# Audio tower: ScalarE makes part of the fp16 high halves by a second gelu pass

## The chip, the cores and the metric

The kernel is one launch on one core of a Trainium2 chip. Times are device microseconds of that core. TensorE is called PE here, VectorE DVE, ScalarE ACT, GpSimd POOL and SyncE SP, as in the profile.

## The reference, cut to what matters

Four clips of 120,000 samples go through six strided convolutions. After each stands a group norm (32 groups of 4 channels) and a gelu in its tanh form. What follows is attention with 12 heads and an expert layer with top-1 choice.

```python
for (cw, cb, gw, gb), (_, _, s) in zip(conv_params, CONV_LAYERS):   # (128,10,5), 4 x (128,3,2), (128,2,2)
    y = conv(h, cw, stride=s) + cb
    yn = (y - mean_of_group) * rsqrt(var_of_group + EPS) * gw + gb
    h = gelu_tanh(yn)
h = h.transpose @ pw.T + pb                # 749 tokens of 192 per clip
h = h + attention(layernorm(h))
h = h + chosen_expert(layernorm(h))        # 8 experts, exact gelu
```

## The kernel before, in words

All engines run their own program in a loop over the four clips ("batches"). In each, the tower comes first (the convolutions, some 150 us), then five passes of a loop over pairs of heads and a last pair, then the work behind attention ("post"). The experts come once, at the end.

**Layout.** Channels are the 128 partitions. A layer's time axis is laid out in rows of 126 columns: 192 rows in layer 0, then 96, 48, 24, 12, 6. A chunk of 8 rows is 1008 columns.

**Two halves.** The convolutions of layers 1 to 5 are fp16 matmuls that need fp32 accuracy. So each activation is kept as a high half (the gelu's value rounded to fp16) and a low half (value minus high half). A bank of 4 output rows is nine matmuls of 504 columns (`terms`, L1680): six on the high half, then three on the low one. PE waits for the high half of a chunk before the first of the nine, and for the low half before the seventh (`hi_done`, `lo_done`).

**PSUM.** `JOBS[TOWER]` is the list of PE's jobs, and each takes one of four slots in turn. Job n may start when the readers of job n-4 have freed its slot (`slot_free`). A conv job is two banks (8 rows), and ACT copies it out in one go (L950, an "eviction"), which frees the slot.

**Layer 0.** A piece is 8 rows of layer 0. There are 24. ACT takes a piece out of PSUM with the gelu (L966) into one of four fp32 stages and so frees the slot. DVE casts it to the high half (L1154) and subtracts to get the low half (L1156). PE makes three pieces, then one or two conv jobs of layer 1, and so on.

**Layers 1 to 4.** When the group norm's scale and bias are there (`affine_ready`), ACT runs `normalise`: one gelu for each chunk of `NORM_CHUNKS`, in place in SBUF (L879). There are 13 chunks in layer 1 (5, 4, ten times 8 and 7 rows), 7 in layer 2, 4 in layer 3, 2 in layer 4. Only behind its last gelu does ACT's program come to the evictions of the next layer's conv jobs. DVE splits the chunks as they come, copies the halo row (L1147, L1148), then takes `bn_stats` of the evicted outputs (L1288, L1284) and aggregates them (L1069) for the next group norm. Layer 2 is made by seven conv jobs: 4, then five of 8, then 4 rows. Layer 3 is made by four, layer 4 by three, layer 5 by one.

**Tables.** The gelu of the tower and the exponential of attention (L893) are in different tables of ACT, so its program has a table load ahead of each.

Of the kernel before, what the change touches and what calls it, by code (L numbers as in the profile page):

```python
# [27 lines left out]
COLS, PITCH = 125, 126  # L28
# [154 lines left out]
def readers(phase, engine):  # L183
# [7 lines left out]
STAGES = 4  # L191


COUNTS = {
    "ps_full": tuple(len(JOBS[f]) for f in PHASES),
    "act_freed": tuple(readers(f, ACT_ENGINE) for f in PHASES),
# [5 lines left out]
    "channel_stats": (1, CONV_LAYERS - 1, 0, 0, 1),  # L202
    "affine_ready": (1, CONV_LAYERS - 1, 0, 0, 1),
    "norm_done": (0, sum(len(c) for c in NORM_CHUNKS.values()), 0, 0, 0),
    "hi_done": (0, len(SPLITS), 0, 0, 0),
    "lo_done": (0, len(SPLITS), 0, 0, 0),
    "halo_done": (0, 4, 0, 0, 0),
    "xn_ready": (0, 1, 0, 0, 1),
# [98 lines left out]
def audio_tower(nc, ins, out):  # L307
# [8 lines left out]
    with ctx:  # L316
# [532 lines left out]
        def _(act):  # L849
# [19 lines left out]
            def normalise(layer, b):  # L869

                wait(act, "affine_ready", TOWER, layer, b)
                r = 0
                for rows in NORM_CHUNKS[layer]:
                    src = ys[layer][:, r * PITCH:(r + rows) * PITCH]
                    dst = src
                    if layer == 5:
                        src = src.rearrange("p (r c) -> p r c", c=PITCH)[:, :, 0:COLS]
                        dst = h5t.rearrange("p (c r) -> p r c", r=rows)
                    a.activation(dst, src, ACT.Gelu_apprx_tanh, bias=affine[:, 1:2], scale=affine[:, 0:1]  # L879
                                 ).then_inc(S["norm_done"], 1)  # L880
                    r += rows
# [57 lines left out]
            with act.Fori(0, BATCH) as b:  # L939
                layer = 0  # L940
                for g, n, kind, args in jobs_of(TOWER):
                    if kind == "conv":
                        if args[0] > 1 and args[1] == 0:
                            normalise(args[0] - 1, b)
                        layer, r, cut = args
                        wait(act, "ps_full", TOWER, n + 1, b)
                        rows = cut[0]
                        dst = ys[layer][:, r * PITCH:(r + sum(cut)) * PITCH]
                        src = slot(g).rearrange("p (k n) -> p k n", k=2)[:, 0:len(cut), 0:rows * PITCH]
                        a.activation(dst.rearrange("p (k n) -> p k n", k=len(cut)), src, ACT.Identity,  # L950
                                     scale=1.0 / WSCALE).then_inc(S["act_freed"], 1)
                    elif kind == "conv0":
                        j, i = args
                        if args == (0, 0):
                            wait(act, "affine_ready", TOWER, 0, b)

                            wait(act, "scratch_stored", TOWER, 0, b)
                        wait(act, "ps_full", TOWER, n + 1, b)
                        piece = 3 * j + i
                        if piece >= STAGES:  # L960

                            had_it = (0, piece - STAGES)
                            wait(act, "hi_done", TOWER, SPLITS.index(had_it) + 1, b)
                            wait(act, "lo_done", TOWER, SPLITS.index(had_it) + 1, b)
                        src = slot(g).rearrange("p (m n) -> p m n", m=2)[:, :, 0:4 * PITCH]
                        a.activation(stage[:, piece % STAGES, :].rearrange("p (m n) -> p m n", m=2), src,  # L966
                                     ACT.Gelu_apprx_tanh,
                                     bias=affine[:, 1:2], scale=affine[:, 0:1]).then_inc(S["act_freed"], 1)
                    elif kind in ("q", "k", "v", "s"):
                        attention_job(TOWER, g, n, kind, args, b)  # L970
                    else:
                        assert kind == "xtr"
                        if layer == 5:
                            normalise(5, b)
                            layer = None
                        wait(act, "ps_full", TOWER, n + 1, b)
                        a.activation(xt_parts[:, args[0], :], bank(g, 0).bitcast(fp16)[:, 0:TOK], ACT.Copy
                                     ).then_inc(S["act_freed"], 1)
                with act.Fori(0, PAIRS - 1) as pr:
                    for g, n, kind, args in jobs_of(PAIR):  # L980
                        attention_job(PAIR, g, n, kind, args, b, pr)
                for g, n, kind, args in jobs_of(LAST_PAIR):
                    attention_job(LAST_PAIR, g, n, kind, args, b)
                for g, n, kind, args in jobs_of(POST):
                    wait(act, "ps_full", POST, n + 1, b)
                    a.activation(xnt1[0:D1, 0:TOK], slot(g)[0:D1, 0:TOK], ACT.Copy).then_inc(S["act_freed"], 1)


            def take_hidden(j, par):
# [19 lines left out]
        def _(dve):  # L1009
# [140 lines left out]
            def split(unit, b):  # L1150

                src, high, low = split_views(*unit)
                n = SPLITS.index(unit) + 1
                v.tensor_copy(high, src).then_inc(S["hi_done"], 1)  # L1154
                dve.wait_ge(S["hi_done"], at("hi_done", TOWER, n, b))
                v.tensor_tensor(low, src, high, ALU.subtract).then_inc(S["lo_done"], 1)  # L1156

            def wait_split(unit, b):
                wait(dve, "hi_done", TOWER, SPLITS.index(unit) + 1, b)
                wait(dve, "lo_done", TOWER, SPLITS.index(unit) + 1, b)  # L1160

            def attention_job(phase, n, kind, args, b, pr=None):
# [284 lines left out]
        def _(pe):  # L1447
# [213 lines left out]
            with pe.Fori(0, BATCH) as b:  # L1661
                for n, (kind, args, who) in enumerate(JOBS[TOWER]):
# [11 lines left out]
                    elif kind == "group":  # L1674
                        wait(pe, "channel_stats", TOWER, args[0], b)
                        last = t.matmul(bank(g, 0)[:, 0:2], group_avg[:, :], ms[:, :], start=True, stop=True)
                    elif kind == "conv":
                        layer, r, cut = args
                        taps = 2 if layer == 5 else 3
                        parts = [a.rearrange("p (r c) -> p r c", c=PITCH) for a in hs[layer - 1]]  # L1680

                        terms = [(tap, w, 0) for tap in range(taps) for w in (0, 1)]
                        terms += [(tap, 0, 1) for tap in range(taps)]
                        for k, c in enumerate(cut):
                            need = 2 * (r + c) - 2 + taps - 1
                            if need >= ROWS[layer - 1]:
                                wait(pe, "halo_done", TOWER, layer, b)
                                need = ROWS[layer - 1] - 1
                            unit = split_unit_of(layer - 1, need)
                            wait(pe, "hi_done", TOWER, SPLITS.index(unit) + 1, b)  # L1690
                            for tap, w, x in terms:
                                if (tap, w, x) == (0, 0, 1):
                                    wait(pe, "lo_done", TOWER, SPLITS.index(unit) + 1, b)
                                f = 2 * r + tap
                                last = t.matmul(bank(g, k)[:, 0:c * PITCH].rearrange("p (r c) -> p r c", c=PITCH),  # L1695
                                                cwt[layer][:, w, tap, :], parts[x][:, f:f + 2 * c - 1:2, :],
                                                start=(tap, w, x) == terms[0], stop=(tap, w, x) == terms[-1])
                            r += c
                    elif kind == "embed":
                        if args[0] == 0:  # L1700
                            wait(pe, "norm_done", TOWER, COUNTS["norm_done"][1], b)
                        tiles = range(4) if args[0] == 0 else range(4, TT)
                        for q, i in enumerate(tiles):
                            m = tile_rows(i)
                            last = t.matmul(bank(g, q // 2)[0:m, (q % 2) * D:(q % 2 + 1) * D],
                                            h5t[:, 128 * i:128 * i + m], pwt[:, :], start=True, stop=True)
                    else:
                        assert kind == "xtr"
                        if args[0] == 0:
                            wait(pe, "xn_ready", TOWER, 1, b)  # L1710
                        for i in range(TT):
                            m = tile_rows(i)
                            last = t.transpose(bank(g, 0).bitcast(fp16)[:, 128 * i:128 * i + m],
                                               xn_parts[0:m, i, args[0], :], ident_h[0:m, 0:m])
# [142 lines left out]
```

## Time and profile before

| | us |
|---|---|
| median of 3 runs | 1816.24 (1814.69 to 1819.27) |
| the profiled execution: its time, its span | 1816.93, 1815.3 |
| PE busy | 1464.7 (81%) |
| DVE busy | 1034.3 (57%) |
| ACT busy | 754.8 (42%) |
| POOL busy | 348.8 (19%) |

The busy shares are means over stages with different limits. The tower is about a third of the span; its first batch lies between 37 and 199 us, with layer 0 up to 101 us and the normalisation of layer 1 from 105.68 us on. The granted clock is TensorE's, as a share of 2.4 GHz.

### The profile page before, as it was taken

To read this page: it belongs to the slowest core of one execution; us is meant where nothing else is said; L and a number is where in the kernel's file an instruction comes from. 1 tells how busy PE (TensorE), PEld (TensorE's weight loads), DVE (VectorE), ACT (ScalarE), POOL (GpSimd) and SP (SyncE) were. 2 spreads that over 40 slices of the span, in tenths; PEclk is the share of its full clock that TensorE was granted. 3 is DMA by queue.
4 is the path that set the end of the run, shared out by engine and by line. 5 is a ranking of instruction groups with operands and counts; after the bars stand their busy time and mean duration, and the time that the engine had idled before them with its cause. 6 is when DMAs were issued, how large, how long until landed. Compare 5 with 4: busy or idle time off the path is not lost.

```text
span 1815.3 us, 32241 instructions
## 1 busy us (share of the span) xinstructions
PE 1464.7 (81%) x10013; PEld 1019.8 (56%) x10014; DVE 1034.3 (57%) x2346; ACT 754.8 (42%) x1456; POOL 348.8 (19%) x390
## 2 busy tenths in 40 slices
PE   4975699998864899989747999898559999159997
PEld 3433477784433677753325777743347778137775
DVE  5987445558884445578964545598744546212221
ACT  2654355525642455435624555265435552012231
POOL 2000134300001334100002333000013331512111
PEclk7987699998986999989878999899769999579999
DMA  4300121210000221110002121100024332621110
GB/s 104 112 1 1 35 60 43 59 36 12 1 1 5 64 59 43 35 38 1 1 1 59 44 59 43 39 1 1 1 57 108 85 86 69 209 56 47 48 50 17
DMA packets 105852, 81.31 MB, mean 45 GB/s; under 512 B 57842, under 2 KB 96267, under 8 KB 105747
## 3 DMA queue, kind: packets, MB, share of 16 engines
q1 hardware_dynamic: 99988, 70.65, 15.5%
q0 software_dynamic: 5760, 9.36, 1.7%
q8 instruction: 54, 0.88, 0.2%
q14 instruction: 50, 0.41, 0.1%
HBM read 34.66 MB, written 18.38 MB: 29 GB/s over the span
## 4 chain that ended last, share of the span: by engine, by line
issue 50%; PE 30%; POOL 7%; DMA 4%; SPq 3%; DVE 3%; ACT 2%; POOLq 0%; DVEq 0%; ACTq 0%
PE ps L1649 5%; PE ps L1591 5%; PE ps L1802 4%; DMA arena<-arena 3%; PE ps L1635 3%; PE ps L1623 3%; PE ps L1782 2%; PE ps L1783 2%; POOL arena L765 2%; PE ps L1598 1%; POOL slot_scratch L824 1%; POOL arena L767 1%; SPq L587 1%; ACT arena L911 1%; PE ps L1790 1%
## 5 line engine op out<-in xcount | busy, mean ns | idle before, releaser
L1695 PE MATMUL ps<-arena,cwt 128*128 128x504 f16 (+2 forms) x1776 | 396.3, 387 | 62.1 <-DVE arena L1154 61.8
L1695 PEld LDWEIGHTS ps<-arena,cwt 128*128 128x128 f16 x1776 | 181.1, 104 | 268.3 <-DVE arena L1154 69.2
L1176 DVE TENSOR_REDUCE nmax<-ps 128x1 f32<-128x128 f32 (+5 forms) x288 | 176.9, 614 | 195.7 <-PE ps L1626 195.7
L1649 PE MATMUL ps<-arena 128*128 128x64 f32 (+2 forms) x2016 | 260.1, 269 | 9.1 <-DVE arena L1184 5.0
L1649 PEld LDWEIGHTS ps<-arena 128*128 128x128 f32 (+2 forms) x2016 | 241.9, 189 | 26.0 <-issue 17.8
L1156 DVE TENSOR_TENSOR arena<-arena 128x1008 f16<-128x1008 f32 (+4 forms) x200 | 227.0, 1135 | 6.9
L1184 DVE COPY arena<-ps 128x512 f32<-128x512 f32 (+4 forms) x288 | 156.1, 542 | 85.8 <-PE ps L1635 81.4
L893 ACT ACTIVATE arena<-ps,nmax 128x128 f32<-128x128 f32 (+5 forms) x288 | 180.8, 628 | 44.1 <-DVE nmax L1176 43.3
L1623 PE MATMUL ps<-arena 128*128 128x512 f16 (+6 forms) x780 | 164.6, 314 | 42.4 <-DMA arena<-arena 21.5
L1635 PE MATMUL ps<-ident,arena 128*128 128x128 f32 (+2 forms) x1008 | 165.8, 282 | 10.6 <-ACT arena L934 5.7
L950 ACT ACTIVATE arena<-ps 128x1008 f32<-128x1008 f32 (+1 forms) x112 | 96.3, 867 | 179.4 <-PE ps L1695 179.4
L934 ACT ACTIVATE arena<-ps,rinv 128x64 f32<-128x64 f32 (+1 forms) x288 | 91.0, 316 | 162.2 <-PE ps L1649 159.1
L879 ACT ACTIVATE arena<-arena,affine 128x1008 f32<-128x1008 f32 (+5 forms) x108 | 113.2, 1125 | 92.8 <-DVE affine L1092 92.8
L1154 DVE CAST arena<-arena 128x1008 f16<-128x1008 f32 (+4 forms) x200 | 128.2, 641 | 28.2 <-ACT arena L879 16.1
L1635 PEld LDWEIGHTS ps<-ident,arena 128*128 128x128 f32 (+2 forms) x1008 | 109.7, 144 | 49.2 <-ACT arena L934 38.4
L756 POOL TENSOR_TENSOR tmp<-tmp,neg_half 128x1 f32<-128x1 f32 x25 | 13.9, 555 | 625.7 <-DVE tmp L1082 625.7
L1623 PEld LDWEIGHTS ps<-arena 128*128 128x128 f16 (+2 forms) x780 | 76.1, 118 | 76.2 <-DMA arena<-arena 24.8
L1288 DVE BATCH_NORM_STATS2 bn<-arena 128x6 f32<-128x500 f32 (+1 forms) x180 | 103.0, 630 | 19.8 <-ACT arena L950 19.7
L966 ACT ACTIVATE arena<-ps,affine 128x1008 f32<-128x1008 f32 x96 | 107.2, 1193 | 0.6 <-DVE arena L1156 0.4
L992 ACT ACTIVATE arena<-ps 128x768 f32<-128x768 f32 x31 | 25.2, 812 | 195.4 <-PE ps L1783 195.4
L765 POOL TENSOR_TENSOR arena<-arena,ones_col 128x750 f16<-128x750 f32 x40 | 57.4, 1435 | 189.5 <-ACT arena L911 189.5
L1591 PE MATMUL ps<-arena,w_parts 128*128 128x375 f16 x288 | 69.0, 353 | 9.4 <-ACT arena L893 6.5
(249 smaller groups left out, 2060.5 us busy)
## 6 DMA issues: line engine op xcount, KB each, us to landing
arena<-arena SPq DMA_DIRECT2D x96, 187.5 KB, 3.0
arena<-arena SPq DMA_DIRECT2D x96, 93.8 KB, 2.6
slot_scratch<-empty_slot SPq DMA_DIRECT2D x1, 5775.0 KB, 19.1
arena<-in_L_ffn_w SPq DMA_DIRECT2D x8, 576.0 KB
arena<-in_L_ffn_w SPq DMA_DIRECT2D x8, 384.0 KB
arena<-slot_scratch SPq DMA_DIRECT2D x31, 96.5 KB, 1.9
arena<-slot_scratch SPq DMA_DIRECT2D x31, 96.0 KB, 2.0
xa<-in_x POOLq DMA_DIRECT2D x5, 468.8 KB, 4.3
```

What stands on the lines that cost most here:

```text
L879: a.activation(dst, src, ACT.Gelu_apprx_tanh, bias=affine[:, 1:2], scale=affine[:, 0:1]).then_inc(S["norm_done"], 1)
L893: a.activation(prob[k % PROBS][0:m, 0:128 * i + m], slot(g)[0:m, 0:128 * i + m], ACT.Exp, bias=nmax[0:m, k_:k_ + 1], accum_out=rsum[0:m, k ...
L966: a.activation(stage[:, piece % STAGES, :].rearrange("p (m n) -> p m n", m=2), src, ACT.Gelu_apprx_tanh, bias=affine[:, 1:2], scale=affine ...
L1154: v.tensor_copy(high, src).then_inc(S["hi_done"], 1)
L1156: v.tensor_tensor(low, src, high, ALU.subtract).then_inc(S["lo_done"], 1)
L1176: v.reduce_max(nmax[0:m, k_:k_ + 1], slot(g)[0:m, 0:128 * i + m], AX.X, negate=True).then_inc(S["smax_done"], 1)
L1184: v.tensor_copy(probt[k % 2][:, 0:w, 0:m], src[:, 0:w, 0:m]).then_inc(S["dve_freed"], 1)
L1591: last = t.matmul(bank(g, k)[:, 0:TOK // 2], weights, x, start=m == 0, stop=m == len(terms) - 1)
L1623: last = t.matmul(slot(g)[0:m, lo:hi], q, keys[:, lo:hi], start=a == 0, stop=a == len(terms) - 1 and not diagonal)
L1635: last = t.transpose(slot(g)[0:kk, 128 * c:128 * c + m], prob[k % PROBS][0:m, 128 * c:128 * c + kk], ident[0:m, 0:m])
L1649: last = t.matmul(slot(g)[0:m, Z_AT:Z_AT + DH], probt[k % 2][0:kk, c, 0:m], vt[0:kk, c, DH * hh:DH * hh + DH], start=c == 0, stop=c == i)
L1695: last = t.matmul(bank(g, k)[:, 0:c * PITCH].rearrange("p (r c) -> p r c", c=PITCH), cwt[layer][:, w, tap, :], parts[x][:, f:f + 2 * c - 1 ...
```

## The change

ACT makes the high half of some chunks itself: a gelu pass with fp16 output straight into the high half, ahead of the pass with fp32 output that it makes anyway. DVE then only subtracts. `hi_engine` says who does it: in layer 0 ACT for pieces 0, 1, 2 and every third one from 3 on (10 of 24), in layers 1 to 4 ACT for chunks 0, 2, 4 and so on (7 of 13, 4 of 7, 2 of 4, 1 of 2). The semaphore `hi_done` becomes two, `hi_act` and `hi_dve`, and PE waits for both. At the end of a batch ACT gets a gelu of one column, whose result nobody reads.

```diff
+def hi_engine(layer, piece):
+    if layer == 0:
+        return ACT_ENGINE if piece < 3 or piece % 3 == 0 else DVE_ENGINE
+    return DVE_ENGINE if piece % 2 else ACT_ENGINE
+def highs(engine, unit):
+    return sum(hi_engine(*u) == engine for u in SPLITS[:SPLITS.index(unit) + 1])
...
+                    elif hi_engine(layer, piece) == ACT_ENGINE:
+                        a.activation(split_views(layer, piece)[1], src, ACT.Gelu_apprx_tanh, bias=affine[:, 1:2],
+                                     scale=affine[:, 0:1]).then_inc(S["hi_act"], 1)
                     a.activation(dst, src, ACT.Gelu_apprx_tanh, bias=affine[:, 1:2], scale=affine[:, 0:1]
                                  ).then_inc(S["norm_done"], 1)
...
                             had_it = (0, piece - STAGES)
-                            wait(act, "hi_done", TOWER, SPLITS.index(had_it) + 1, b)
                             wait(act, "lo_done", TOWER, SPLITS.index(had_it) + 1, b)
                         src = slot(g).rearrange("p (m n) -> p m n", m=2)[:, :, 0:4 * PITCH]
+                        if hi_engine(0, piece) == ACT_ENGINE:
+                            a.activation(split_views(0, piece)[1],
+                                         src.rearrange("p m (k c) -> p m k c", c=PITCH), ACT.Gelu_apprx_tanh,
+                                         bias=affine[:, 1:2], scale=affine[:, 0:1]).then_inc(S["hi_act"], 1)
...
+                a.activation(spare[:, 30:31], ones_col[:, :], ACT.Gelu_apprx_tanh)
...
-                v.tensor_copy(high, src).then_inc(S["hi_done"], 1)
-                dve.wait_ge(S["hi_done"], at("hi_done", TOWER, n, b))
+                if hi_engine(*unit) == DVE_ENGINE:
+                    v.tensor_copy(high, src).then_inc(S["hi_dve"], 1)
+                    dve.wait_ge(S["hi_dve"], at("hi_dve", TOWER, highs(DVE_ENGINE, unit), b))
+                else:
+                    dve.wait_ge(S["hi_act"], at("hi_act", TOWER, highs(ACT_ENGINE, unit), b))
                 v.tensor_tensor(low, src, high, ALU.subtract).then_inc(S["lo_done"], 1)
...
-                            wait(pe, "hi_done", TOWER, SPLITS.index(unit) + 1, b)
+                            wait(pe, "hi_act", TOWER, highs(ACT_ENGINE, unit), b)
+                            if highs(DVE_ENGINE, unit):
+                                wait(pe, "hi_dve", TOWER, highs(DVE_ENGINE, unit), b)
```

ACT between the last eviction of layer 1 and the first of layer 2, before (L879 is the gelu of `normalise`, L950 the eviction):

```order
L879 ACTIVATE arena<-arena,affine 128x630 [waits affine_ready]
L879 ACTIVATE arena<-arena,affine 128x504
L879 ACTIVATE arena<-arena,affine 128x1008 x10
L879 ACTIVATE arena<-arena,affine 128x882
L516 REGISTER_ALU
L950 ACTIVATE arena<-ps 128x504 [waits ps_full]
```

The same place now (L893 is the added pass, L895 the old one, L966 the eviction):

```order
L893 ACTIVATE arena<-arena,affine 128x630 [waits affine_ready]
L895 ACTIVATE arena<-arena,affine 128x630
L895 ACTIVATE arena<-arena,affine 128x504
L893 ACTIVATE arena<-arena,affine 128x1008
L895 ACTIVATE arena<-arena,affine 128x1008 x2
...
L893 ACTIVATE arena<-arena,affine 128x882
L895 ACTIVATE arena<-arena,affine 128x882
L529 REGISTER_ALU
L966 ACTIVATE arena<-ps 128x504 [waits ps_full]
```

Where 13 gelus stood ahead of the first eviction, 20 stand now.

ACT at the head of the loop over the batches, now (L982 is the added pass in layer 0, L985 the old one; L529 holds the waits):

```order
L529 ISA [waits affine_ready]
L529 ISA [waits scratch_stored]
L982 ACT_TABLE_LOAD
L982 ACTIVATE arena<-ps,affine 128x2x4x126 [waits ps_full]
L985 ACTIVATE arena<-ps,affine 128x1008
```

And at the end of the loop's body, now (L1007 is the gelu of one column):

```order
L1005 ACTIVATE arena<-ps 64x750
L1007 ACT_TABLE_LOAD
L1007 ACTIVATE spare<-ones_col 128x1
L955 REGISTER_ALU
L955 COMPARE_AND_BRANCH
```

The load at the loop's end is new. The one at its head, behind the wait for `affine_ready`, stands where it stood before.

## Rows read from the trace of the kernel before

**Rows 1.** Who PE waited for, whole span: us in total, times, longest.
```profile
PE ps L1676 <- DVE ms L1071: 62.3, 20, 5.8
PE ps L1695 <- DVE arena L1154: 61.8, 20, 3.4
```
**Rows 2.** Layer 0, batch 0: us; busy PE, PEld, DVE, ACT, POOL; clock; DMA share; GB/s.
```profile
38.00:102.00 64.00, 58.12 (x256) 24.32 (x256) 57.98 (x75) 39.20 (x38) 0.00 (x0) 0.92 0.34 106
```
**Rows 3.** Timeline of DVE, layer 1 normalised: start us, us, what [idle before].
```profile
106.62 0.49 DVE L1154 CAST arena<-arena 128x630 f16<-128x630 f32 x1 [0.98 <-ACT arena L879]
107.15 0.81 DVE L1156 TENSOR_TENSOR arena<-arena 128x630 f16<-128x630 f32 x1
...
136.38 0.53 DVE L1069 BATCH_NORM_AGGREGATE mv<-bn 128x2 f32<-128x84 f32 x1
```
**Rows 4.** Timeline of PE, the same stretch.
```profile
107.17 24.43 PE L1695 MATMUL ps<-arena,cwt 128*128 128x252 f16 x117 [3.25 <-DVE arena L1154]
```
**Rows 5.** Timeline of ACT, the same stretch.
```profile
105.68 13.82 ACT L879 ACTIVATE arena<-arena,affine 128x630 f32<-128x630 f32 x13 [4.49 <-DVE affine L1092]
119.40 2.36 ACT L950 ACTIVATE arena<-ps 128x504 f32<-128x504 f32 x3
122.07 1.01 ACT L950 ACTIVATE arena<-ps 128x1008 f32<-128x1008 f32 x1 [0.31 <-PE ps L1695]
125.90 1.01 ACT L950 ACTIVATE arena<-ps 128x1008 f32<-128x1008 f32 x1 [2.81 <-PE ps L1695]
...
131.64 0.59 ACT L950 ACTIVATE arena<-ps 128x504 f32<-128x504 f32 x1 [0.90 <-PE ps L1695]
```
**Rows 6.** Forms between 105 and 170 us: count, busy us, mean ns.
```profile
L879 ACT ACTIVATE arena<-arena,affine 128x1008 f32<-128x1008 f32 x15 | 17.1, 1214 | 0.0
L1154 DVE CAST arena<-arena 128x1008 f16<-128x1008 f32 x15 | 10.2, 678 | 0.0
...
L879 ACT ACTIVATE arena<-arena,affine 128x882 f32<-128x882 f32 x3 | 3.3, 1111 | 0.0
L879 ACT ACTIVATE arena<-arena,affine 128x630 f32<-128x630 f32 x3 | 2.7, 913 | 15.8 <-DVE affine L1092 15.8
...
L879 ACT ACTIVATE arena<-arena,affine 128x504 f32<-128x504 f32 x3 | 2.4, 793 | 0.0
```
**Rows 7.** Two reads of one PSUM slot by ACT, fp16 then fp32 out.
```profile
203.71 0.89 ACT L909 ACTIVATE arena<-ps,bqkv 128x750 f16<-128x750 f32 x1 [3.85 <-PE ps L1591]
204.50 0.88 ACT L911 ACTIVATE arena<-ps,bqkv 128x750 f32<-128x750 f32 x1
```
**Rows 8.** Stretches of 1 us, PE idle; the granted clock stands third from the end.
```profile
133.00:134.00 1.00, 0.00 (x0) 0.00 (x0) 1.00 (x3) 0.00 (x0) 0.00 (x0) 0.85 0.00 0
134.00:135.00 1.00, 0.00 (x0) 0.00 (x0) 1.00 (x2) 0.00 (x0) 0.00 (x0) 0.50 0.00 0
```
**Rows 9.** Timeline of PE, first conv job of layer 1, batches 0 and 1.
```profile
44.45 5.92 PE L1695 MATMUL ps<-arena,cwt 128*128 128x504 f16 x18 [2.29 <-DVE arena L1154]
...
423.03 5.69 PE L1695 MATMUL ps<-arena,cwt 128*128 128x504 f16 x18 [2.36 <-DVE arena L1154]
```
**Rows 10.** Timeline of PE, the convolution of layer 3.
```profile
141.23 13.27 PE L1695 MATMUL ps<-arena,cwt 128*128 128x252 f16 x63 [3.24 <-DVE arena L1154]
```
**Rows 11.** Timeline of DVE, the same stretch: the aggregation behind the last bn_stats.
```profile
155.94 0.37 DVE L1069 BATCH_NORM_AGGREGATE mv<-bn 128x2 f32<-128x48 f32 x1
```
**Rows 12.** Timeline of ACT in layer 0, batch 0, and its start in batch 1.
```profile
38.80 6.60 ACT L966 ACTIVATE arena<-ps,affine 128x1008 f32<-128x1008 f32 x6
...
55.58 1.01 ACT L950 ACTIVATE arena<-ps 128x1008 f32<-128x1008 f32 x1 [0.92 <-PE ps L1695]
...
416.79 5.52 ACT L966 ACTIVATE arena<-ps,affine 128x1008 f32<-128x1008 f32 x5
```
**Rows 13.** ACT in batch 1; then all loads of L966: ns min/median/max.
```profile
415.49 1.28 ACT L966 ACT_TABLE_LOAD   x1 [10.94 <-DVE affine L1092]
...
L966 ACT ACT_TABLE_LOAD  x4: 1283/1283/1283, 37.5 to 1173.1; - x4
```

More of the change, by code:

```diff
@@ L204 @@
     "norm_done": (0, sum(len(c) for c in NORM_CHUNKS.values()), 0, 0, 0),
-    "hi_done": (0, len(SPLITS), 0, 0, 0),
+    "hi_act": (0, sum(hi_engine(*u) == ACT_ENGINE for u in SPLITS), 0, 0, 0),
+    "hi_dve": (0, sum(hi_engine(*u) == DVE_ENGINE for u in SPLITS), 0, 0, 0),
     "lo_done": (0, len(SPLITS), 0, 0, 0),
@@ L872, in normalise @@
                 r = 0
-                for rows in NORM_CHUNKS[layer]:
+                for piece, rows in enumerate(NORM_CHUNKS[layer]):
                     src = ys[layer][:, r * PITCH:(r + rows) * PITCH]
@@ L1152, in split @@
                 src, high, low = split_views(*unit)
-                n = SPLITS.index(unit) + 1
-                v.tensor_copy(high, src).then_inc(S["hi_done"], 1)
-                dve.wait_ge(S["hi_done"], at("hi_done", TOWER, n, b))
+                if hi_engine(*unit) == DVE_ENGINE:
[3 more added lines that the diff above has]
+                    dve.wait_ge(S["hi_act"], at("hi_act", TOWER, highs(ACT_ENGINE, unit), b))
                 v.tensor_tensor(low, src, high, ALU.subtract).then_inc(S["lo_done"], 1)
             def wait_split(unit, b):
-                wait(dve, "hi_done", TOWER, SPLITS.index(unit) + 1, b)
+                if hi_engine(*unit) == ACT_ENGINE:
+                    wait(dve, "hi_act", TOWER, highs(ACT_ENGINE, unit), b)
                 wait(dve, "lo_done", TOWER, SPLITS.index(unit) + 1, b)
```

## The prediction

> **What bounds the kernel now.** I read the waits first, then the busy time by stretch, then the timeline of each engine over the first batch's tower. In the waits [rows 1] two groups of 20 belong to the tower: 62.3 us in which PE waits for DVE's statistics and 61.8 us for DVE's casts. So DVE looks like the engine to relieve. The stretches show where that holds. In layer 0 [rows 2] PE is busy 58.12 of 64.00 us and DVE 57.98. Once PE has begun its first conv job at 44.45 it never waits there, so PE sets the pace and DVE, though nearly full, is just behind. In the normalisation of layer 1, DVE sets the end: from the first cast at 106.62 to the aggregation at 136.38 it has no gap (first cast and aggregation stand in [rows 3]), while PE was done at 107.17 + 24.43 = 131.60 [rows 4] and then waited. ACT has its 13 gelus done at 105.68 + 13.82 = 119.50 [rows 5]. That is before the fifth of seven conv jobs of layer 2 needs the first one's slot: evictions of full jobs follow each other by 125.90 - 122.07 = 3.83 us, so a matmul of 504 columns takes 3.83 / 18 = 0.213 us, and jobs five to seven are 45 of them, 9.57 us. They began at 131.55 - 9.57 = 121.97, and the first slot was free by about 120.
>
> **The change, part by part.** Sums are made against the profiled execution, 1816.93 us (span 1815.3), 0.7 us over the median of 1816.24.
>
> *Layer 1, the casts that go.* DVE loses seven of 13 casts: about 0.5 + 5 x 0.68 + 0.6 = 4.5 us [rows 3, 6]. If DVE stayed the bound, this would be the gain.
>
> *Layer 1, the passes that come.* ACT gets seven passes: 0.913 + 5 x 1.214 + 1.111 = 8.09 us of durations [rows 6]. Back to back they overlap: 13 gelus have 0.913 + 0.793 + 10 x 1.214 + 1.111 = 14.96 us of durations and take 13.82 [rows 5], 0.095 us for each. That leaves 7.43 us. No row shows this gelu with an fp16 output. The nearest are two reads of one slot, 0.89 us in fp16 and 0.88 in fp32 [rows 7], so I take no difference. The last gelu ends at 119.50 + 7.43 = 126.93, and the first eviction, about 0.5 us later, at 127.45. The fifth job needs that slot. PE, ready at 121.97, waits 5.5 us. This is what is queued behind the added passes: seven evictions on ACT, on them PE's jobs five to seven, on these DVE's `bn_stats`.
>
> *The clock.* After PE stopped at 131.6 the granted clock went from 1.00 to 0.85 in the stretch 133 to 134 and to 0.50 from 134 on, which is 1.2 instead of 2.4 GHz [rows 8]. So I expect it at 1.2 GHz when job five begins. What the way back costs: 18 matmuls after such a stop took 5.69 to 5.92 us against 3.83 [rows 9], a loss of about 1.9. After the stop at 107.17, 117 matmuls took 24.43 us [rows 4]; the last 99 are 99 x 0.213 = 21.05 us, so the first 18, of half width, took 3.4 against 1.9, a loss of 1.5. I take 1.7, and 0 as the lower bound.
>
> *The end of the stage.* PE ends at 127.45 + 9.57 + 1.7 = 138.7. DVE has caught up by then. Behind a PE that ends last, the aggregation comes 155.94 - (141.23 + 13.27) = 1.44 us later [rows 10, 11]. So it comes at 140.16 instead of 136.38: +3.8 us a batch, and +2.1 if the clock costs nothing.
>
> *The early start.* PE may begin on the high half that ACT makes at about 106.6, not at 107.17. But the low half of chunk 0 now waits for ACT's second pass, to 107.4, and for 0.81 us of subtraction [rows 3], while six matmuls at 1.2 GHz last 1.3 us. So PE stops again in front of the seventh, and bank 2 ends where it ended. I count 0. The same holds in layers 2 to 4.
>
> *Layers 2 to 4.* They have four conv jobs, three and one behind them, so all slots are free and no eviction is waited for. ACT's added four, two and one passes end before PE does. The last chunk's halves come up to 0.5 us later in layer 3. I take +0.3 us for all three, with -0.5 and +1.5 as bounds.
>
> *Layer 0, start.* ACT runs gelus in PSUM at a step of (6.60 - 1.19) / 5 = 1.08 us [rows 12]. The first conv job is job 6 and needs the slot of piece 2, which is free after the sixth pass now, not after the third: 38.80 + 6.60 = 45.4 against 44.45 before, +1.0 us. In batches 1 to 3 the first conv job began later anyway, 423.03 - 416.79 = 6.24 us after ACT [rows 9, 12]; there it is +0.4.
>
> *Layer 0, inside.* Removed casts give nothing, since PE sets the pace. ACT makes one more pass, 1.08 us, for every three pieces, where it had 0.92 us of idle time plus 0.1 of overlap ahead of the eviction at 55.58 [rows 12]. Evictions come 0.05 to 0.1 us late, and behind single conv jobs PE waits for them: +0.15 us a batch, 0 to +1.
>
> *The table load.* Before each tower 1.28 us of table load stand behind `affine_ready`, on the path in each of four batches [rows 13]. ACT's order shows that this load stays at the head of the loop, and that the gelu of one column adds a second one at its end. That one runs in ACT's idle time ahead of the head, 10.94 us in batch 1, so it costs nothing. It also gives nothing: the load at the head is an instruction in the program and runs whatever table is in. The Trainium skill ("ScalarE: Activation LUTs", step-by-step on the table-load gate) says that the compiler has put a load in front of an activation if its set isn't active, which read alone would promise that the load goes. The page "ScalarE activation tables: per-element evaluation and per-set limits" (table sets in the compiler) says that loads are placed per block; by this rule the loop's body is given its own, and ACT's order agrees.
>
> *Waits.* PE's extra waits stand ahead of matmuls that queue behind others, and cost nothing while PE's queue is full.
>
> *Sum.* Layer 1: 4 x 3.8 = 15.2. Layer 0: 1.0 + 3 x 0.4 + 4 x 0.15 = 2.8. Layers 2 to 4: 1.2. Together +19.2 us: 1836.1 in the profile's terms, 1835 as a median.
>
> **The rivals.**
> - *The clock doesn't fall in the new stop, or costs nothing.* For it: the stop of 5.5 us is short, and its place against the fall seen 2.2 us after 131.6 may differ. Against: [rows 8]. Then 4 x 1.7 less: 1828.5.
> - *The touch works.* The load at the head is passed over, or takes no time, where the gelu table is already in. No row shows a load of a table that is in; all four took 1283 ns. Then three batches gain 1.28 us each: 1831.
> - *Faster: DVE's relief wins in layer 1.* If ACT's added passes cost so little that the first eviction comes before 121.97, PE ends at 131.6, the aggregation 1.44 us later at 133.0, and each batch gains 3.4 us: with layer 0 as above, about 1816 - 13.6 + 2.8 = 1805. The balance is where PE ends at 134.9: at added ACT work of some 5.4 us without the clock's loss and 3.7 with it. I reckon with 7.4, so the passes would have to cost half of what these rows say.
> - *Only the sizes differ.* If the fp16 pass with rows of 126 columns is slower than the fp32 one by 10%, layer 1 grows by 0.8 us a batch: 1838.5 and more, up to 1842 with layer 0.
>
> **How the numbers follow.** Chances: the forecast, with its sizes, 0.64; no loss by the clock 0.14; the touch works 0.10; slower sizes 0.06; faster 0.03; effects that cancel, within 0.3%, 0.03. A change of 0.3% (5.4 us) is about what a measurement of this kernel can tell from none. Slower by more than that: 0.94. The range reaches from 1823 (no loss by the clock, and layer 0 without its start) to 1842.
>
> **What would show it.** In the changed kernel's timeline of ACT, 20 passes after layer 1's affine take about 21.2 us. PE's conv stretch of layer 2 is in two parts with a stop near 5.5 us between job four and five, ended by an ACT eviction, and the clock is 0.50 at the start of the second part. PE waits for ACT evictions for some 22 us in all, where before there are none of that kind. The table load at the head of each batch is there, 1283 ns long, eight of the gelu kind instead of four, and ACT's first gelu begins 1.3 us behind the affine. DVE's casts fall by 24 a batch. It is wrong if PE's jobs five to seven follow without a stop, or if the head's loads are gone.

## The result, and the profile after

The changed kernel takes 1842.91 us, the median of 4 runs (1841.21 to 1847.80). The kernel before takes 1815.92 in the runs beside them. The ratio is 1.015, with an interval of 1.0126 to 1.0174: 27 us slower (23 to 32), where 19.2 were forecast. 1842.9 lies 0.9 us above the range's upper end. In the profiled execution (1841.21 us, span 1839.6) it is +24.3 us of span. A total can hide which of its terms were wrong, so each is looked up below.

The page's busy row after; against before DVE is down by 54 us and ACT up by 101:

```profile
PE 1488.9 (81%) x10013; PEld 1022.9 (56%) x10014; DVE 980.3 (53%) x2250; ACT 856.2 (47%) x1560; POOL 348.4 (19%) x390
```

PE's waits after (us in total, times, longest). The first two answer to [rows 1]; the third line is new:

```profile
PE ps L1700 <- DVE ms L1092: 50.0, 20, 2.8
PE ps L1721 <- ACT arena L893: 44.0, 16, 2.8
PE ps L1721 <- ACT arena L966: 17.4, 4, 5.3
```

PE's timeline after, layer 1 normalised and layer 2 convolved, batches 0 and 1. It answers to [rows 4]:

```profile
107.83 1.44 PE L1721 MATMUL ps<-arena,cwt 128*128 128x252 f16 x6 [2.73 <-ACT arena L893]
109.57 13.89 PE L1721 MATMUL ps<-arena,cwt 128*128 128x252 f16 x66 [0.30 <-DVE arena L1179]
128.79 11.31 PE L1721 MATMUL ps<-arena,cwt 128*128 128x504 f16 x45 [5.33 <-ACT arena L966]
...
492.69 15.17 PE L1721 MATMUL ps<-arena,cwt 128*128 128x252 f16 x66 [0.30 <-DVE arena L1179]
511.92 12.58 PE L1721 MATMUL ps<-arena,cwt 128*128 128x504 f16 x45 [4.06 <-ACT arena L966]
```

The one stretch of 117 matmuls is now in three parts: six matmuls on the high half from ACT, 66 more, and behind a stop of 5.33 us the 45 of jobs five to seven. ACT's timeline, the same stretch of batch 0, and DVE's aggregation behind it, show what ends the stop. They answer to [rows 5] and [rows 3, 11]:

```profile
106.86 0.91 ACT L893 ACTIVATE arena<-arena,affine 128x630 f16<-128x630 f32 x1 [4.41 <-DVE affine L1113]
...
126.97 1.11 ACT L895 ACTIVATE arena<-arena,affine 128x882 f32<-128x882 f32 x1
127.98 3.25 ACT L966 ACTIVATE arena<-ps 128x504 f32<-128x504 f32 x4
```
```profile
141.54 0.53 DVE L1090 BATCH_NORM_AGGREGATE mv<-bn 128x2 f32<-128x84 f32 x1
```

ACT's 20 passes run from 106.86 to 128.08, 21.22 us. Only then comes its first eviction, and PE starts again 0.81 us after that one began. PE ends at 128.79 + 11.31 = 140.10, and the aggregation follows 1.44 us later.

The granted clock at PE's new stop, in stretches of 1 us (columns: from and to, length, PE busy with its instructions, clock, DMA share, GB/s); batch 0, then batch 1:

```profile
127.00:128.00 1.00, 0.00 (x0) 1.00 0.00 0
128.00:129.00 1.00, 0.21 (x1) 0.81 0.00 0
129.00:130.00 1.00, 1.00 (x3) 0.50 0.00 0
132.00:133.00 1.00, 1.00 (x6) 0.99 0.00 0
...
510.00:511.00 1.00, 0.00 (x0) 0.95 0.00 0
...
517.00:518.00 1.00, 1.00 (x5) 0.64 0.00 0
518.00:519.00 1.00, 1.00 (x6) 1.00 0.00 0
```

In batch 0 the clock falls from 1.00 to 0.50, to 1.2 GHz, only while PE starts again, and is back at 132, after 3.2 us of matmuls. In batch 1 it falls during the stop, and comes back only shortly before 518, after 5.8 us of matmuls. The same 45 matmuls take 11.31 us there and 12.58 here, against the forecast's 9.57 at 2.4 GHz.

Stage lengths tell where the rest is. They are differences between DVE's writes of `affine`, summed over the four batches (us; "elsewhere" is the span less these, all in code that the change leaves alone):

| kernel | layer 0 | layer 1 | layers 2-4 | elsewhere | span |
|---|---|---|---|---|---|
| before | 274.1 | 136.3 | 174.6 | 1230.3 | 1815.3 |
| after | 278.5 | 155.6 | 179.2 | 1226.4 | 1839.6 |
| touch at the end | 274.4 | 136.3 | 174.5 | 1230.7 | 1815.8 |
| touch at the head | 272.2 | 136.3 | 177.9 | 1228.5 | 1814.8 |
| only layer 1 | 274.8 | 152.4 | 173.8 | 1228.6 | 1829.5 |
| the same, PE kept warm | 274.1 | 145.4 | 177.7 | 1233.2 | 1830.3 |
| only layer 0 | 281.3 | 136.3 | 176.4 | 1235.7 | 1829.7 |
| layer 0's start | 278.5 | 136.3 | 179.6 | 1229.1 | 1823.5 |
| layer 0's inside | 273.8 | 136.6 | 178.1 | 1228.9 | 1817.3 |
| only layers 2-4 | 274.3 | 136.3 | 176.7 | 1226.8 | 1814.0 |
| all but layer 0 | 274.1 | 152.7 | 179.1 | 1227.0 | 1832.9 |
| early evictions | 273.1 | 138.0 | 176.2 | 1229.2 | 1816.5 |
| whole change mended | 274.3 | 138.1 | 178.9 | 1226.9 | 1818.1 |
| four passes, early eviction | 273.0 | 128.6 | 182.6 | 1232.0 | 1816.2 |
| PE filled | 273.3 | 135.5 | 169.4 | 1228.2 | 1806.4 |
| both | 273.8 | 127.8 | 170.8 | 1229.8 | 1802.2 |

Two things are to be seen. Layer 1 carries most of the loss. And stages that a kernel's edit doesn't touch move by up to 8 us in sum, so small differences in one stage's sum, or in the span of one execution, show nothing.

### The profile page after: what moved, and what is told of

Same layout as the page of the kernel before. It is cut to its first block, busy times and chain, and to the rows that moved or that the text cites. A ratio compares the mean times of both kernels' runs of the same rounds, so it can differ in the third digit from the quotient of the medians.

```text
span 1839.6 us, 32421 instructions
## 1 busy us (share of the span) xinstructions
PE 1488.9 (81%) x10013; PEld 1022.9 (56%) x10014; DVE 980.3 (53%) x2250; ACT 856.2 (47%) x1560; POOL 348.4 (19%) x390
## 4 chain that ended last, share of the span: by engine, by line
issue 51%; PE 30%; POOL 7%; DMA 4%; SPq 3%; DVE 3%; ACT 2%; POOLq 0%; DVEq 0%; ACTq 0%
PE ps L1673 5%; PE ps L1615 5%; PE ps L1828 3%; DMA arena<-arena 3%; PE ps L1647 3%; PE ps L1659 3%; PE ps L1808 2%; PE ps L1809 2%; POOL arena L778 2%; PE ps L1622 1%; POOL slot_scratch L837 1%; POOL arena L780 1%; SPq L600 1%; ACT arena L927 1%; PE ps L1816 1%
## 5 line engine op out<-in xcount | busy, mean ns | idle before, releaser
L1721 PE MATMUL ps<-arena,cwt 128*128 128x504 f16 (+2 forms) x1776 | 417.3, 399 | 73.4 <-ACT arena L893 44.0
L950 ACT ACTIVATE arena<-ps,rinv 128x64 f32<-128x64 f32 (+1 forms) x288 | 90.8, 315 | 162.7 <-PE ps L1673 158.9
L966 ACT ACTIVATE arena<-ps 128x1008 f32<-128x1008 f32 (+1 forms) x112 | 95.4, 866 | 123.2 <-PE ps L1721 123.0
L895 ACT ACTIVATE arena<-arena,affine 128x1008 f32<-128x1008 f32 (+5 forms) x108 | 116.7, 1123 | 16.6 <-DVE affine L1113 16.6
L985 ACT ACTIVATE arena<-ps,affine 128x1008 f32<-128x1008 f32 x96 | 108.5, 1202 | 0.0
L893 ACT ACTIVATE arena<-arena,affine 128x1008 f16<-128x1008 f32 (+3 forms) x56 | 62.7, 1120 | 64.3 <-DVE affine L1113 64.3
L927 ACT ACTIVATE arena<-ps,bqkv 128x750 f32<-128x750 f32 x48 | 42.5, 885 | 75.2 <-PE ps L1659 39.4
```

## The experiments

My theory: ACT's evictions stand in its program behind the added passes, and PE's jobs wait for them; the clock's fall adds to it. Rivals: the passes themselves or contention cost; the table touch matters; the loss is in layer 0. The edits are shown shortened to the lines that matter, and dots stand for what is left out.

**The touch alone**, at the loop's end as in the change, and instead at its head. Both are before plus one line:

```
+ a.activation(spare[:, 30:31], ones_col[:, :], ACT.Gelu_apprx_tanh)   # end of the loop's body
```


> The kernel before with the gelu of one column at a batch's end, nothing else. My theory: the load at the head of the loop stays, 1283 ns behind the affine in each of four batches, and the added load lies in idle time: same time as before, within 1 us. Rival (the touch works): three batches gain 1.28 us each, 3.8 us less. Second rival (the touch is among the causes of the 24 us): 1 us or more slower.

```
  with act.Fori(0, BATCH) as b:
+     a.activation(spare[:, 30:31], ones_col[:, :], ACT.Gelu_apprx_tanh)
```


> The kernel before with the same gelu of one column as ACT's first instruction in the loop's body, ahead of the wait for the affine. My theory: a load is placed once per block, so it moves in front of the wait; ACT is idle there (4.9 us in batch 0, 10.9 later): four times 1.28 us less, about 1811. Rival: the time between affine and first conv job is set by another engine, and the gain is under 2 us.

At the end: 1817.49, ratio 0.9993 (0.9982 to 1.0004). At the head: 1815.13, 0.9985 (0.9975 to 0.9995). ACT's timelines at the start of batch 1, touch at the end, then at the head:

```profile
405.09 1.28 ACT L988 ACT_TABLE_LOAD   x1
...
416.00 1.28 ACT L966 ACT_TABLE_LOAD   x1 [9.42 <-DVE affine L1094]
417.30 5.52 ACT L966 ACTIVATE arena<-ps,affine 128x1008 f32<-128x1008 f32 x5
```
```profile
408.94 1.28 ACT L941 ACT_TABLE_LOAD   x1 [3.62 <-issue]
...
417.67 6.60 ACT L967 ACTIVATE arena<-ps,affine 128x1008 f32<-128x1008 f32 x6 [7.24 <-PE ps L1672]
```

At the end, the head's load is still there and takes its 1.28 us though the gelu table is in. This is the Trainium skill's rule of loads placed per block ("ScalarE activation tables: per-element evaluation and per-set limits", table sets in the compiler), and the trace agrees. At the head the load moves into idle time, and the first gelu waits for PE instead. So the whole gain is 0.15% or 2.7 us (0.9 to 4.5), not the 5.1 that were expected of four loads. In the profiled execution layer 0's stage is 1.5 us shorter in batch 0 and 0.0 to 0.3 in the others.

**Layer 1 alone**: the changed kernel with ACT's share in one layer, without the touch.

```
- return DVE_ENGINE if piece % 2 else ACT_ENGINE
+ return ACT_ENGINE if layer == 1 and piece % 2 == 0 else DVE_ENGINE
```


> The changed kernel with ACT's added passes in layer 1 alone (7 chunks; no pass in layers 0 and 2 to 4, no touch). Theory A, the stop of PE behind the fourth conv job and the slow clock after it carry the loss: layer 1's stage is 4.0 to 5.1 us longer a batch, 16 to 20 us in all, 1832 to 1836. Rival B, the loss above the forecast's 3.8 in batches 1 to 3 came over from layer 0's changed timing: 15 us in all, 1831. Rival C, the loss is spread over all layers: under 10 us.

1831.47, ratio 1.0072 (1.0056 to 1.0087). Layer 1's stages are 38.12, 38.06, 38.17 and 38.01 us against 34.06 to 34.08: +4.0 in every batch, where 3.8 was forecast. PE's timeline in batch 1:

```profile
511.38 11.31 PE L1721 MATMUL ps<-arena,cwt 128*128 128x504 f16 x45 [5.32 <-ACT arena L966]
```

This is batch 0 of the changed kernel again. So the 12.58 us and the shorter stop of its batch 1 don't come from layer 1's own edit.

**The same with PE kept warm**, that is busy, so that the clock stays up: PE repeats the nine matmuls of job four's second bank twice, which changes no result and shortens its stop (again over the kernel with layer 1 alone).

```
+ for again in range(2 if (layer, r, k) == (2, 24, 1) else 0):
+     for tap, w, x in terms:
+         last = t.matmul(...)
```


> The kernel with ACT's passes in layer 1 alone, in which PE repeats the last bank of layer 2's fourth conv job twice (18 matmuls of 504 columns, 3.83 us at 2.4 GHz, same result), so that it works through most of the stop. Theory A: job five starts at the same time, on ACT's eviction, but at 2.4 GHz, so layer 1's stage costs only 2.2 us a batch over the kernel before, 9 us in all, about 1825. Rival: if the slow matmuls behind the stop don't come from the stop, the time is that of layer 1 alone, 1832 to 1836, or more if the repeats are in the way.

1829.96, ratio 1.006 (1.0044 to 1.0076). PE's timeline in batch 1:

```profile
502.00 3.99 PE L1727 MATMUL ps<-arena,cwt 128*128 128x504 f16 x18
507.48 9.73 PE L1721 MATMUL ps<-arena,cwt 128*128 128x504 f16 x45 [1.50 <-ACT arena L966]
```

PE begins job five at the same place behind ACT's passes, but at 2.4 GHz or nearly so: 9.73 us instead of 11.31. Layer 1 costs +2.2 us a batch instead of +4.0, so the split of the 3.8 into queue and clock (2.1 and 1.7) holds. Yet the whole time is hardly better, and not the 1825 expected: in the profiled executions the 7.0 us gained in layer 1 come back as 3.9 in layers 2 to 4 and 4.6 elsewhere (this kernel's profiled execution is 2.1 us over its median).

**The queue taken away**: as layer 1 alone, but three evictions are written between the passes.

```
+ if layer == 1 and piece in (8, 10, 12):
+     evict(first + (8, 10, 12).index(piece), ...)
```


> ACT's seven passes in layer 1 alone, but ACT evicts the first three conv jobs of layer 2 between its gelus, behind chunks 8, 10 and 12, not behind the last. Theory A, the queue behind the passes is the cause: the same added work on ACT, but the slot of the first job is free before PE wants it, no stop, and layer 1's stage is at most 1 us longer than before (ACT's last gelu comes at 22.7 us, DVE's seven us of statistics behind it), so 1816 to 1820. Rival: the passes themselves are the cost (ACT's pace per chunk, or contention for SBUF), and the time stays at 1831.

1818.63, ratio 1.0003 (0.9994 to 1.0013). PE's and DVE's timelines in batch 1:

```profile
488.84 23.74 PE L1737 MATMUL ps<-arena,cwt 128*128 128x252 f16 x111 [0.31 <-DVE arena L1194]
```
```profile
506.73 0.69 DVE L1190 CAST arena<-arena 128x1008 f16<-128x1008 f32 x1 [0.71 <-ACT arena L907]
507.45 1.21 DVE L1194 TENSOR_TENSOR arena<-arena 128x1008 f16<-128x1008 f32 x1
508.84 1.08 DVE L1194 TENSOR_TENSOR arena<-arena 128x882 f16<-128x882 f32 x1 [0.19 <-ACT arena L907]
```

The stop is gone, and with it the loss: +0.44 us a batch is left. All seven passes are still there, so in themselves they cost no more than that; the order of ACT's program does. But nothing is gained from DVE's relief either, since DVE now waits for ACT's gelus up to the last chunk.

**Layer 0 alone**, then only its first three pieces, then only the pieces inside:

```
+ return ACT_ENGINE if layer == 0 and (piece < 3 or piece % 3 == 0) else DVE_ENGINE   # layer 0
+ return ACT_ENGINE if layer == 0 and piece < 3 else DVE_ENGINE                       # start
+ return ACT_ENGINE if layer == 0 and piece > 5 and piece % 3 == 0 else DVE_ENGINE    # inside
```


> The changed kernel with ACT's passes in layer 0 alone (10 of 24 pieces, no touch). Theory: layer 0's stage is longer as in the changed kernel, 0.4 to 1.9 us a batch, and the others are as before: 1817 to 1822. What came over from layer 0 to layer 1 in the changed kernel needs a stop in layer 1, which isn't there, so layer 1 stays at 34.1 us a batch. Rival: relief of DVE pays in layer 0, and the stage is shorter.

> ACT's added passes for pieces 0, 1 and 2 of layer 0 alone. With all ten pieces, layer 0's stage was 1.6 to 1.95 us longer a batch. Theory: that is the start. The first conv job needs the slot of piece 2, freed by ACT's sixth pass and not its third (0.8 to 1.0 us), and the clock comes back to 2.4 GHz about 1.1 us of work later, so nearly all of it is here: 1.5 to 1.9 us a batch in layer 0, 6 to 7.6 us in the sum of its stages. Rival: the start costs the forecast's 0.4 to 1.0, and the rest is ACT's pace inside the layer: 2.5 us in the sum.

> ACT's added passes for pieces 6, 9, 12, 15, 18 and 21 of layer 0 alone, none at its start. Theory: an eviction behind every third piece comes 0.05 to 0.1 us late, and layer 0's stage grows by 0.1 to 0.3 us a batch, about 1 us in all: not to be told from the kernel before. Rival: the rest of layer 0's loss is here, 1 us or more a batch, 1822.

Layer 0 alone: 1831.04, ratio 1.0065 (1.0049 to 1.0082). Start: 1825.14, 1.0038 (1.0025 to 1.0051). Inside: 1817.49, 1.0003 (0.9994 to 1.0013). The inside costs nothing, the start does, and layer 0 is far over the forecast. But start and inside come to 7 and 0.5 us against 12, a gap of 4 to 5 us that is at the edge of the errors. Piece 3 is ACT's in the change and in neither of the two parts, and no run has it alone. PE's timeline with layer 0 alone, first conv job of batch 2, with the granted clock of the stretches; then before:

```profile
808.91 6.75 PE L1721 MATMUL ps<-arena,cwt 128*128 128x504 f16 x18 [1.22 <-ACT arena L985]
```
```profile
808.90:812.00 3.10, 3.09 (x8) 0.50 0.00 0
812.00:814.00 2.00, 2.00 (x7) 0.50 0.00 0
814.00:815.00 1.00, 1.00 (x5) 0.74 0.00 0
```
```profile
801.80 5.69 PE L1695 MATMUL ps<-arena,cwt 128*128 128x504 f16 x18 [2.32 <-DVE arena L1154]
```
```profile
801.80:805.00 3.20, 3.20 (x10) 0.64 0.00 0
805.00:806.00 1.00, 1.00 (x4) 0.50 0.00 0
806.00:807.00 1.00, 1.00 (x6) 0.93 0.00 0
```

The table load that opens the batch began at 800.50 here and at 794.23 before, so the job starts 8.41 us behind it instead of 7.57: +0.84. And it lasts 1.06 us longer, at 1.2 GHz nearly throughout, where before a part ran faster. Together 1.9, which is what the stage is longer by (70.5 against 68.6). Batches 0 and 1 have jobs of 6.31 and 6.79 us. With the start alone, batch 2's job stands 8.03 us behind its load, +0.46 (0.4 were forecast), and lasts 5.95 us; the rest of the +0.84 is ACT's first gelu, which waits 0.40 us for PE in the kernel with layer 0 alone.

Of +14.4 us of span layer 0 holds 7.2, layers 2 to 4 hold 1.8 and code elsewhere 5.4: every batch's attention and remainder is 233.4 to 233.5 us instead of 232.1 to 232.4. The clock explains at most half of that. Added up over stretches of 2 us, the time at 1.2 GHz is 35.5 us a batch instead of 34.4, and 1.1 us at half the speed loses 0.6 us of work. In the kernel called "whole change mended" the same stretch of batch 3 is shorter, 231.05 us, with 36.5 us at 1.2 GHz.

**Layers 2 to 4 alone, and all but layer 0**:

```
+ return ACT_ENGINE if layer > 1 and piece % 2 == 0 else DVE_ENGINE     # layers 2 to 4
```


> The changed kernel with ACT's passes in layers 2 to 4 alone. In the changed kernel these stages were 4.5 us longer over four batches, where the forecast had 1.2. Theory: it is their own cost, the later low halves and the later halo row, so 4 to 5 us here, about 1821. Rival: it was the clock's state left by the stop in layer 1, and here they cost 1 us or less.


```
  if layer == 0:
-     return ACT_ENGINE if piece < 3 or piece % 3 == 0 else DVE_ENGINE
+     return DVE_ENGINE                                                 # the rest as in the change
```


> The whole change less ACT's passes in layer 0 (layers 1 to 4 and the touch stay). Theory A: layer 0's timing set the clock's state in layer 1, so layer 1's stage is 4.0 us longer than before in every batch and not 5.1, layers 2 to 4 cost 0 to 2 us in all, and the kernel is near 1830. Rival B: layer 1 at 5.1 us comes from the passes in layers 2 to 4 or the touch, and stays: 1835 or more.

Layers 2 to 4 alone: 1816.33, ratio 0.9991 (0.9982 to 1.0001), nothing where 4 to 5 us were expected. All but layer 0: 1832.7, ratio 1.0076 (1.0059 to 1.0092), and layer 1's stages are back at 38.17, 37.94, 38.44 and 38.10. So what makes them 39.1 to 39.2 in batches 1 to 3 of the changed kernel is the edit in layer 0, a stage earlier. Layers 2 to 4 stay at 179.1, as in the changed kernel, so what these stages have over before does not come from layer 0's edit.

**The whole change with both waits mended**: pieces 0 to 3 back to DVE, three evictions early in layer 1.

```
- return ACT_ENGINE if piece < 3 or piece % 3 == 0 else DVE_ENGINE
+ return ACT_ENGINE if piece > 5 and piece % 3 == 0 else DVE_ENGINE
+ if layer == 1 and piece in (8, 10, 12): evict(...)
```


> The whole change with both suspected waits taken away: in layer 0 ACT makes high halves only from piece 6 on (pieces 0 to 3 are DVE's again), and in layer 1 the first three evictions stand behind chunks 8, 10 and 12. 20 of 24 added passes a batch stay. Theory A: the two waits are all of it, so 1816 to 1820. Rival B: the passes have a cost of their own, spread out: 1825 or more.

1818.39, ratio 1.000 (0.999 to 1.001). The two places on ACT are the whole loss, within 0.1%; the other 20 of 24 added passes a batch cost nothing that can be measured. In layer 1 this is shown for the order alone, with every pass kept. In layer 0 the passes themselves went, four of them, so there the queue is the explanation that fits the rows, and not shown apart from the passes.

**A better split**: touch at the head, only chunks 4, 6, 8 and 10 of layer 1 on ACT, one eviction early.

```
+ return ACT_ENGINE if layer == 1 and piece in (4, 6, 8, 10) else DVE_ENGINE
+ if layer == 1 and piece in (9,): evict(...)
```


> A version meant to win: the touch at the head of the loop's body, ACT's passes in layer 1 for four chunks alone (4, 6, 8, 10), and the first conv job of layer 2 evicted behind chunk 9. By the terms measured so far: DVE loses 4 x 0.71 us of casts in layer 1 and stays the bound, ACT ends its gelus at 18.8 us and isn't waited for, so 2.7 us less a batch, 10.8 in all, and 3 for the touch: about 1804. Rival: PE's or ACT's pace takes the bound at once and layer 1 gives nothing: 1815.

1817.56, ratio 0.9993 (0.9984 to 1.0002). Layer 1 is shorter by 1.9 us in each batch, as DVE's casts leave its path, and the sum is still nothing, not the 1804 expected: 7.7 us gained there, 7.9 lost in layers 2 to 4. PE's timeline of the next convolution, batch 1, this kernel and before:

```profile
514.49 0.59 PE L1716 MATMUL ps<-ms,group_avg 128*128 128x2 f32 x2 [3.51 <-DVE ms L1108]
518.32 14.31 PE L1738 MATMUL ps<-arena,cwt 128*128 128x252 f16 x63 [3.24 <-DVE arena L1191]
```
```profile
515.72 0.59 PE L1676 MATMUL ps<-ms,group_avg 128*128 128x2 f32 x2 [5.53 <-DVE ms L1071]
519.55 13.27 PE L1695 MATMUL ps<-arena,cwt 128*128 128x252 f16 x63 [3.24 <-DVE arena L1154]
```

The same 63 matmuls come 1.2 us earlier and take 1.04 us more, at the lower clock for longer (7.2 us instead of 5.6 in this stage, added up over stretches of 1 us). This stage takes 19.2 to 20.5 us in these kernels, also where nothing near it was edited: with the touch at the head it is 20.55 us in batch 0, with 7.8 us at the lower clock, and 19.4 in the others. Here all four batches are near the upper end.

**PE filled**: around the matmul that averages the statistics PE does others whose result nobody reads, so that it doesn't idle there; over the kernel with the touch at the head, and over the last one.

```
+ for again in range((0, 9, 20, 7, 7, 0)[layer]):     # (0, 9, 12, 7, 7, 0) over the last one
+     t.matmul(bank(g, 1)[:, 0:4 * PITCH], cw0t[:, 0, :], xt[:, 0:4, :]...)
  wait(pe, "channel_stats", ...); last = t.matmul(..., group_avg, ms)
+ for again in range((0, 11, 11, 11, 11, 0)[layer]): ...
```


> The kernel before with the touch at the head, in which PE does matmuls whose results nobody reads (504 columns, into the unused bank of the group job's slot) while it waits for statistics and for the first high half of layers 1 to 4. Theory: PE's slow matmuls at the start of layers 3, 4 and 5's convolutions (some 1.0, 2.0 and 1.0 us a batch) are the clock's alone, so they go, and the stages of layers 2 to 4 are 3 to 5 us shorter a batch: about 1799. The stage of layer 1 stays, DVE sets it. Rival: the slow stretch is the cost of starting a job, not of idling before it, and nothing moves: 1815.

> The same filling in the version with ACT's passes for four chunks of layer 1, which was 1.9 us a batch shorter in layer 1 and gave it all back in layers 2 to 4 (1.1, 0.6 and 0.2 us a batch), with the clock at 1.2 GHz for 7.3 to 7.8 us of layer 2's stage where it had been 5.4 to 5.8. Theory: with the clock held up, layer 1's gain stays: 7 us under the filled kernel, about 1792. Rival: the give-back has another cause and stays: the two are equal.

The first: 1812.32, ratio 0.9978 (0.996 to 0.9995), with runs spread from 1807.18 to 1821.79. The second: 1802.95, ratio 0.9911 (0.9897 to 0.9926), 14.4 us under the kernel before by the medians (13 to 19 by the interval) and 40 under the changed one: it beats both. PE's timeline of it, batch 1:

```profile
504.82 2.71 PE L1717 MATMUL ps<-xt,cw0t 105*128 105x504 f16 x12
509.00 0.39 PE L1720 MATMUL ps<-ms,group_avg 128*128 128x2 f32 x2 [1.47 <-DVE ms L1108]
509.25 3.56 PE L1723 MATMUL ps<-xt,cw0t 105*128 105x504 f16 x11
512.63 10.39 PE L1747 MATMUL ps<-arena,cwt 128*128 128x252 f16 x54
523.87 2.09 PE L1747 MATMUL ps<-arena,cwt 128*128 128x504 f16 x9 [0.86 <-issue]
```

PE's pause of 3.51 us is 1.47, the one of 3.24 is gone, and the next 54 matmuls run at 2.4 GHz but for some 1.3 us at their start (clock 0.72 from 512.60 to 515.00, then 1.00). In this stage the time at the lower clock is 3.1 us in batch 1 and nothing in the other three. Layer 1's gain now stays (127.8 against 136.3), and layers 2 to 4 take 170.8 instead of 182.6. The two times lie 13 and 11 us over what was expected (1799 and 1792).

## Why the prediction was right in direction and too small

*Layer 1, passes and queue (15.2): right.* The fp16 pass has the price of the fp32 one, as assumed: for 1008 columns both take 1213 ns in the mean out of SBUF, and 1187 and 1200 ns in the median out of PSUM. The last gelu ends 21.22 us after the first began (21.25 forecast), PE stops for 5.33 us (5.5), the aggregation comes 1.44 us after PE. Alone, this layer adds 16.1 us in its stages. Taking the queue away takes it back; the passes alone cost 0.44 us a batch at most. That was shown by experiment.

*The clock (1.7): right once, wrong as a constant.* At 11.31 us for 45 matmuls it is 1.74 in batch 0, as it is with layer 1 alone in batch 1. In the changed kernel it is 3.0 in batch 1, and the stages of batches 2 and 3 (39.19 and 39.22 us, against 39.13) say the same of them. That is why layer 1 comes to 19.3 and not 15.2. Without layer 0's edit it is back at +3.9 to +4.4 a batch: shown. What in the timing of layer 0 decides whether the clock is back 3 us after PE starts again or 6 is open.

*Layer 0, start (1.0 + 3 x 0.4): the step that failed.* The delay itself was right, the slot of piece 2 behind the sixth pass: batch 0 starts its first conv job 8.03 us behind the table load instead of 6.94, +1.09, and the other batches +0.59, +0.67 and +0.46. The step that failed is to price layer 0's edit by this delay alone, and to let the clock's loss be the same 1.7 whatever comes before. I moved the job and left its length, and I left out that the move changes when the clock comes back later on. PE's timeline after, which answers to [rows 9]:

```profile
44.80 6.60 PE L1721 MATMUL ps<-arena,cwt 128*128 128x504 f16 x18 [1.22 <-ACT arena L985]
```

It takes 6.60 us and not 5.92; in batches 1 to 3 it takes 5.54, 5.88 and 5.92 where it took 5.69. Alone, the start costs 7 us (4.5 to 9.3) and layer 0 12 (9 to 15), where 2.8 were forecast. In the whole change layer 0's edit costs 13 us: the ratio is 1.0150 with it and 1.0076 without. Without it the rest of the sum was sound, 16.4 us forecast and 14 measured (11 to 17). In the profiled executions with and without it, its part is +4.4 us in layer 0's stages and +2.9 in layer 1's, through the longer clock loss; layers 2 to 4 and the code elsewhere hold +0.1 and -0.6. The rest of the 13 lies between single executions and medians, and no row shows it. The parts add up within their errors (by the ratios 13.1 + 11.8 - 1.6 = 23.3, each with an error of 2 to 3 us, against 23 to 32 for the whole), which leaves room for a few us more.

*Layer 0, inside (0.15 a batch): right*, nothing that can be measured. *The early start: right.* PE begins on ACT's high half 0.5 us earlier, does six matmuls and stops for 0.30. *Layers 2 to 4 (1.2):* alone nothing that can be measured, +2.1 us in the stages; in the changed kernel, and in the one without layer 0's edit, they take +4.5, and "elsewhere" takes -3.9 and -3.3, which no term had.

*The table load: right*, at the end it neither costs nor gives. The rival that it works is refuted there. Of the other rivals, "the clock costs nothing" came near only where PE was kept busy up to a stop of 1.50 us (9.73 us against 9.57); "DVE's relief wins" needs another order: four passes and an eviction between them give 1.9 us a batch in layer 1. The rival on sizes named the fp16 pass, which costs no more than the fp32 one. The range's lower end doesn't follow from its words: the median forecast of 1835, less 4 x 1.7 and the start's 2.2, is 1826 and not 1823. Of the signs that were to show the steps, DVE's casts fell by 96 in 2346 (24 a batch) and the loads of the gelu kind are eight; PE's waits for evictions are 17.4 us and not 22, since in batches 1 to 3 the clock had taken longer over the matmuls ahead of the stop (15.17 us for 66 instead of 13.89), which left less to wait.

What stays open: why unchanged code elsewhere takes 1226 to 1236 us in these kernels, above all why the attention is 1.1 us a batch longer in the kernel with layer 0 alone; whether the 4 to 5 us of layer 0 that neither its start nor its inside has are real, and where they lie; and why the filled kernel's runs spread so widely.

## What to carry to other kernels

Before giving work to an engine with slack, look at what stands behind it in that engine's program and who waits for that: here seven passes on an engine with time to spare cost 4 us a batch because evictions stood behind them, and with three evictions written between them 0.44 us was left. A stop that is added, moved or saved on PE also moves the granted clock, so price the matmuls behind it again, and check the next stages, before a gain counts. Where PE pauses a few us between dense stretches, matmuls that nobody reads may be what lets a gain stay: it was so in one kernel here.

## What the runs showed of the hardware

- A stop of PE costs more than its length, and not always the same: 45 matmuls behind a stop took 11.31 us after one of 5.33 us and 12.58 after one of 4.06, against 9.57 worked out for 2.4 GHz; behind a stop of 1.50 us they took 9.73. The shorter of the two long stops was the dearer one.
- What counted was how long the clock stayed at 1.2 GHz after PE had started again: 3.2 us in the first case and 5.8 in the second. When it had fallen counted for little: in batch 2 of the kernel with all but layer 0 it fell 2.3 us into a stop of 5.20, was back 3.7 us after PE's start, and the 45 matmuls took 11.53 us.
- The lower clock can undo a gain: -1.9 us in one stage came with +1.0 in the next, and with PE busy through its pauses the gain stayed (layer 1's stages at 127.8, layers 2 to 4 at 170.8 instead of 182.6).
- A table load of 1283 ns runs even when its table is in; behind it the first gelu began 1.30 us after the load's start (416.00 and 417.30), so nothing else was added.
